# Four of sixteen mask preloads on ScalarE, filler matmuls in the first five turns, and a new order of the turn

## The reference

```python
x = x + _L0_attn_ref(_layernorm(x), Wq, Wk, Wv, ...)          # delta rule, gates, output gate
x = x + _L0_xattn_ref(_layernorm(x), ctx_1024, ctx_1024, mask, Wq, Wk, Wv, Wo)
x = x + _L0_ffn_ref(_layernorm(x), clip_x, clip_down, w_gate, w_up, w_down)
# inside _L0_xattn_ref:
scores = jnp.einsum('bhqd,bhkd->bhqk', Q, K) / np.sqrt(16)
scores = jnp.where(mask == 0, -jnp.inf, scores)
out = jnp.einsum('bhqk,bhkd->bhqd', softmax(scores), V)
```

## Time and profile before

| | us |
|---|---|
| median of 3 runs | 1278.31 (1277.05 to 1282.93) |
| the profiled execution, own time | 1273.96 |
| its span, first to last instruction | 1272.2 |
| PE busy | 1071.3 (84%) |
| DVE busy | 986.7 (78%) |
| ACT busy | 749.2 (59%) |
| POOL busy | 641.7 (50%) |

### The profile page before, as it was taken

One profiled execution on the slowest core, in us unless ns is written; L12 is line 12 of the kernel. 1 busy time (PEld: TensorE's weight loads), 2 busy tenths in 40 slices (PEclk: granted clock), 3 DMA queues, 4 the chain that ended last, 5 costly groups with the idle time before them and its releaser, 6 DMA issues. The chain is left out here.

```text
span 1272.2 us, 27987 instructions
## 1 busy us (share of the span) xinstructions
PE 1071.3 (84%) x8552; PEld 806.0 (63%) x8626; DVE 986.7 (78%) x2955; ACT 749.2 (59%) x1456; POOL 641.7 (50%) x2360
## 2 busy tenths in 40 slices
PE   5888988684677789999999999999999987875755
PEld 4767766683556567777777777777777645443224
DVE  4989988685766869788888888888888776834985
ACT  5877877432343435675666567566656544444766
POOL 4777775405334744565566556556655654101007
PEclk9988889895557869999999999999999998997989
DMA  6667666546021434353353445335343442205007
GB/s 183 214 199 231 197 208 204 180 90 173 34 84 50 121 88 127 105 150 114 93 151 110 132 123 157 115 94 150 109 138 85 145 103 59 76 26 190 1 1 232
DMA packets 159829, 160.31 MB, mean 126 GB/s; under 512 B 65320, under 2 KB 126656, under 8 KB 159680
## 3 DMA queue, kind: packets, MB, share of 16 engines
q1 hardware_dynamic: 155552, 157.47, 41.7%
q10 hardware_dynamic: 4128, 1.05, 0.4%
HBM read 96.34 MB, written 61.87 MB: 124 GB/s over the span
## 5 line engine op out<-in xcount | busy, mean ns | idle before, releaser
L2142 DVE CUSTOM_DVE_ANT_0 x_psA<-x_psA,x_mask_q 128x256 f32<-128x256 f32 x496 | 201.1, 447 | 82.5 <-PE x_psA L1431 59.2
L1694 ACT ACTIVATE x_PT<-x_psB 128x512 f32<-128x512 f32 x240 | 143.2, 596 | 140.8 <-PE x_psB L1458 133.8
L314 DVE SCALAR_TENSOR_TENSOR a_conv<-a_ps_proj,taps,a_conv 128x253 f32<-128x253 f32 (+2 forms) x288 | 114.9, 470 | 12.5 <-ACT a_conv L381 12.5
L537 PE MATMUL a_ps_proj<-a_hT,wqkv 128*128 128x256 f32 x384 | 104.8, 421 | 11.0 <-DVE a_conv L314 7.8
L1431 PE MATMUL x_psA<-x_Ks,x_Qs 96*128 96x256 bf16 x496 | 97.8, 279 | 13.0 <-DVE x_maxima L2142 12.8
L1458 PE MATMUL x_psB<-x_Qs,x_Ks 98*128 98x256 bf16 x480 | 92.7, 274 | 7.3 <-ACT x_PT L1694 2.5
L537 PEld LDWEIGHTS a_ps_proj<-a_hT,wqkv 128*128 128x128 f32 x384 | 77.1, 212 | 30.2 <-issue 15.9
L2142 DVE DVE_READ_ACCUMULATOR2_ANT x_maxima<- 128x1 f32 x512 | 72.2, 141 | 0.0
L1455 PE MATMUL x_psB<-x_mask_k,x_ident_bf 128*128 128x512 bf16 x167 | 64.8, 388 | 8.5 <-ACT x_PT L1694 7.5
L1472 PE MATMUL x_psO<-x_PT,x_V 128*32 128x256 f32 x1024 | 70.3, 393 | 1.6 <-ACT x_PT L1694 1.6
L1431 PEld LDWEIGHTS x_psA<-x_Ks,x_Qs 96*128 96x128 bf16 x496 | 41.4, 101 | 47.0 <-DVE x_maxima L2142 26.8
(11 more groups left out here) (383 smaller groups left out, 3262.5 us busy)
## 6 DMA issues: line engine op xcount, KB each, us to landing
scratch_keypack<-a_keypack SPq DMA_DIRECT2D x16, 768.0 KB, 4.2
c_keypack<-scratch_keypack SPq DMA_DIRECT2D x16, 768.0 KB, 4.9
x_Ks<-scratch_k_parts SPq DMA_DIRECT2D x192, 64.0 KB, 2.7
matrix<-scratch_taps_copies SPq DMA_DIRECT2D x32, 256.0 KB, 4.0
scratch_k_parts<-x_parts_k SPq DMA_DIRECT2D x32, 192.0 KB, 2.3
scratch_q_parts<-x_parts_q SPq DMA_DIRECT2D x32, 192.0 KB, 2.3
x_Qs<-scratch_q_parts SPq DMA_DIRECT2D x32, 192.0 KB, 3.0
a_x_in<-in_x SPq DMA_DIRECT2D x16, 256.0 KB, 3.9
```

Of the source, the lines that this page charges most:

```text
L314: nc.vector.scalar_tensor_tensor(acc, ps_proj[PROJ_BANK[p]][:, c, 0:L - j], taps[:, p, c, TAPS - 1 - j:TAPS - j], acc, ALU.mult, ALU.add). ...
L537: last = nc.tensor.matmul(ps_proj[PROJ_BANK[p]][:, o], wqkv[:, p, c, o * P:(o + 1) * P], hT[par][:, c], start=c == 0, stop=c == FC - 1)
L1694: nc.scalar.activation(PT[:, k % (2 * GROUP)], bank_B(b, k)[0], ACT.Exp, scale=XD ** -0.5).then_inc(pexp_ready, 1)
L2142: last = nc.vector.tensor_tensor_reduce(bank_A(b, k)[0][:, s], bank_A(b, k)[0][:, s], mask_q[:, t], 1.0, LOWEST, ALU.add, ALU.max, maxima[ ...
```

## The change

Three edits, all in `phase_cx`:

1. `MASKED_BY_ACT` becomes (3, 7, 11, 15). For batches 0 to 13 the L1455 matmul of these four heads is left out, and ACT copies the mask into psB (`kB3`, `kB7`, `kB11`, `kB15`).
2. PE gets filler: the operations `hot0` to `hot13` multiply the identity (read as bf16) by itself, 512 columns, into the bank psO, whose content nobody reads in those turns. `HOT[b][i]` says how many matmuls `hoti` issues for batch b; there are 134 in all, for b below 5. By turn they are 3 in turn 0, then 28, 30, 24 and 40, and 9 in turn 5, ahead of the first `pv0`. They wait for nothing, and nothing waits for them.
3. `C_ORDER` is a new list. All engines' orders change. Some operations get another stage number because the list is cut at another place (`gram0` is now the first of turn n+1 where it stood late in turn n).

```diff
-C_ORDER = [(2, "rv"), (3, "osum3"), (4, "scale"), (5, "mA10"), (2, "delta"), (1, "invx"), (5, "mA11"), (1, "invq"),
...
+C_ORDER = [(2, "r1"), (0, "invb"), (4, "scale"), (3, "mixa"), (5, "mA8"), (4, "oF"), (4, "klow"), (3, "mixb"), (4, "rstdx"),
...
+           (1, "gram0"), (6, "sB10"), (5, "sA10"), (1, "hot11"), (2, "out"), (1, "hot12"), (6, "sB11"), (5, "sA11"),
+           (6, "pv1"), (5, "sA12"), (1, "hot13"), (0, "hot0"), (6, "sB12"), (1, "gram1"), (0, "hot1"), (5, "sA13"),
+           (6, "sB13"), (6, "pv2"), (6, "sB14"), (3, "oT8"), (1, "p1"), (5, "sA14"), (0, "hot2"), (3, "og1"), (5, "sA15"),
+           (6, "sB15"), (4, "vproj"), (5, "maxT"), (6, "pv3"), (4, "sA0"), (0, "hot3"), (3, "og2"), (3, "ctxT"), (4, "Q1st"),
...
+           (4, "sA4"), (6, "wop"), (0, "hot4"), (1, "sqv"), (2, "gelu1"), (5, "eB0"), (5, "eB1"), (6, "ofc"), (3, "khigh"),
+           (5, "eB2"), (3, "oTc"), (5, "kB3"), (5, "eB3"), (1, "ua0"), (5, "eB4"), (1, "w0"), (2, "exp"), (5, "eB5"),
...
+           (2, "logits"), (4, "sA5"), (5, "sB4"), (1, "b0"), (0, "hot5"), (0, "hot6"), (7, "tuh"), (5, "sB5"), (1, "c0"),
+           (0, "hot7"), (5, "sB6"), (1, "state"), (0, "hot8"), (4, "sA6"), (0, "hot9"), (5, "pv0"), (4, "sA7"), (1, "rhs1"),
+           (3, "xT"), (5, "sB7"), (4, "sA8"), (1, "a1"), (3, "qproj"), (5, "sB8"), (1, "b1"), (4, "sA9"), (5, "sB9"),
+           (0, "hot10"), (1, "c1"), (4, "K1st"), (3, "K0st"), (1, "uc0"), (1, "S"), (5, "eB6"), (5, "kB7"), (3, "xTc"),
...
+HOT = ((2, 0, 0, 0, 0, 0, 0, 0, 0, 1, 0, 0, 1, 0),
+       (3, 0, 4, 1, 6, 0, 0, 8, 1, 0, 4, 0, 0, 4),
+       (7, 0, 0, 0, 2, 3, 4, 0, 6, 0, 4, 0, 0, 0),
+       (0, 3, 0, 3, 4, 0, 2, 3, 0, 6, 3, 0, 0, 8),
+       (0, 6, 0, 8, 0, 2, 7, 3, 0, 1, 5, 0, 1, 8))
 
-MASKED_BY_ACT = ()
+MASKED_BY_ACT = (3, 7, 11, 15)
...
+                elif op[:3] == "hot" and b < len(HOT):
+                    pair = ident[:].bitcast(BF16)
+                    for _ in range(HOT[b][int(op[3:])]):
+                        nc.tensor.matmul(psO[:], pair[:, 0:P], pair.unsqueeze(1).broadcast_to([P, 2, L]),
+                                         start=True, stop=True, skip_group_check=True)
```

More of the change, by code:

```diff
@@ L784 @@
 NVB = 2
-C_ORDER = [(2, "rv"), (3, "osum3"), (4, "scale"), (5, "mA10"), (2, "delta"), (1, "invx"), (5, "mA11"), (1, "invq"),
-           (1, "att0"), (4, "oF"), (4, "klow"), (4, "rstdx"), (7, "rstdb"), (4, "qlow"), (3, "ostat"), (5, "mA12"),
[10 rows of a table removed]
-           (3, "st_qp"), (2, "ld_x"), (3, "ld_Q0"), (2, "ld_c"), (1, "ld_hT"), (3, "statx"), (4, "mA5"), (2, "pr1"),
-           (2, "pr2"), (4, "mA6"), (2, "pr3"), (1, "r1"), (0, "invr"), (4, "mA7"), (3, "xnx"), (2, "mixa"), (4, "mA8"),
-           (2, "mixb"), (2, "mixc"), (2, "mix"), (3, "qrest"), (4, "mA9"), (2, "osum"), (5, "sB4"), (1, "c0"), (4, "sA6"),
[9 rows of a table removed]
+C_ORDER = [(2, "r1"), (0, "invb"), (4, "scale"), (3, "mixa"), (5, "mA8"), (4, "oF"), (4, "klow"), (3, "mixb"), (4, "rstdx"),
+           (3, "mixc"), (4, "qrest"), (3, "mix"), (7, "rstdb"), (5, "mA9"), (3, "osum"), (3, "osum3"), (2, "sums0"),
[15 rows of a table added]
+           (2, "ld_x"), (1, "ld_hT"), (3, "st_kp"), (3, "ld_K0"), (3, "st_qp"), (0, "ld_vs"), (3, "proj"), (5, "sB3"),
[8 rows of a table added]
+HOT = ((2, 0, 0, 0, 0, 0, 0, 0, 0, 1, 0, 0, 1, 0),
[4 rows of a table added]
 LOWEST = -3.0e38
-MASKED_BY_ACT = ()
+MASKED_BY_ACT = (3, 7, 11, 15)
 def phase_cx(nc, sems, dram, keep, ident, used, early):
```

## The result

The changed kernel takes 1265.89 us (median of 12 runs, 1257.55 to 1271.04); the kernel before, in 12 runs beside it, 1277.66 us. The ratio is 0.9905, with a 95% interval from 0.9877 to 0.9933. So 12 us were gained where 26.6 were forecast. The profiled execution took 1270.57 us, with a span of 1268.8.

A forecast was written before the change was run, and what follows sets the result against it. The prediction took PE's work to bound the steady turn, and hand-offs between engines, with PE at a low clock, the ramp. Masks 10.6, filler 12 and order 4 us saved gave 1278.31 - 26.6 = 1251.7, rounded to 1252 us; range 1236 to 1276.

The forecast's parts named there:

- Edit 1, the price: Mask matmuls on PE: each one left out saves 0.22 us from start to start, 0.88 us a turn.
- Edit 1, the sum: Masks from ScalarE: 9.7 us over 11 full turns plus a third of 2.6 us, 10.6 us saved in all.
- My count of chains: Ahead of sB3, sB7, sB11, sB15: PE's work between scores covers exponential and copy, 4.1 to 2.6 us against 1.9 to 2.6.
- `proj` to `xT`: Tightest link found in the new order: at least 7.1 us against 7.0 us of PE work, perhaps 0.1 to 0.5 us a turn.
- Edit 2: Filler in the ramp: a higher clock saves 18 us, 6 us of filler is not covered, net 12 us saved.
- Rival B: Only the steady part gains, the ramp keeps its length over DVE, POOL and ACT: 1267, up to 1272 us; chance 0.18.
- E: Filler doesn't lift the clock, its matmuls run at 0.43 us each on PE's queue: 1296 us, slower; chance 0.08.
- C: Most of the ramp's PE time was on the path, pipeline shallower by all 11 us: 1230 us; chance 0.07.
- Edit 3: New order: a shallower pipeline saves 4 of 11 us in ramp and tail; bounds 11 us saved, 4 us lost.
- The sum: Whole kernel: 10.6 + 12 + 4 = 26.6 us saved, from 1278.31 to 1251.7 us, rounded to 1252.
- rival D: Steady turn stays at 44.5 us, a late link or copy stalling PE 0.9 us a turn: 1272 to 1284 us; chance 0.09.
- What the profile was to show: Steady turn 43.6 to 43.9 us with PE busy over 98%; ramp clock near 1.0, about 170 instead of 184.7 us.

The follow-up runs named there:

- e16: The kernel before in its old order, with ScalarE writing the masks of heads 1, 3, 9, 11 and 190 filler matmuls: 1250.27 us, ratio 0.9787.
- e7: The kernel before in its old order with 190 filler matmuls alone, all masks from PE: 1260.8 us, ratio 0.9894.
- e1: The changed kernel with MASKED_BY_ACT empty, new order and filler kept: 1267.46 us, ratio 0.9944.
- e2: The changed kernel without any filler matmul, new order and ScalarE's masks kept: 1275.32 us, ratio 1.0009.
- e3: The kernel before with the new order alone, neither ScalarE's mask copies nor filler: 1281.39 us, ratio 1.0071.
- e9: The changed kernel with no mask at all, neither matmul nor copy, for heads 3, 7, 11, 15 of batches 0 to 13: 1270.51 us.
- e4: The kernel before in its old order, with ScalarE writing the masks of heads 3, 6, 9, 11, no filler: 1268.01 us, ratio 0.9963.
- e5: The kernel before in its old order, with ScalarE writing the masks of heads 3, 6, 9, 11 and 190 filler matmuls: 1250.57 us, ratio 0.9828.
- e17: The kernel before in its old order, with ScalarE writing the masks of heads 1, 3, 6, 9, 11 and filler: 1251.0 us, ratio 0.9795.

## Why the prediction was right or wrong

**What bounds the kernel: right, but one sentence claimed more than it could.** "In the steady part the sum of PE's work is the turn" holds for the kernel before to within the 1.9 us counted above. It doesn't follow that the sum less 0.88 is the next turn. PE busy for 43.96 of 44.5 us says that nobody is late by much, not by how little the others are in time. Here several hand-offs turned out to have less room than the work that was taken away ahead of them.

The reading of the ramp had a slip too: the 41.0 us of its first window begin 4 us ahead of the first evacuation, and the turn took 37.0 us.

**Edit 1, the price: right.** 0.22 us from start to start is confirmed: e16 gives 0.84/4 = 0.21 us a matmul where no wait follows. The figure of the Trainium skill (TensorE: Matmul & The Clock Gate, section Back-to-back issue gap), 131 ns for a matmul with 512 columns in a sustained stream, would give 0.52 us a turn; the measurement decides against it. The same section of the Trainium skill has about 216 ns for such a matmul taken alone at the upper clock, and that is what the runs show even in a stream: twelve filler matmuls of e7, each with its weight load, take 2.76 us, so (2.76 - 0.38)/11 = 0.216 us from start to start.

```profile
398.25 2.76 PE L1516 MATMUL x_psO<-ident 128*128 128x512 bf16 x12
```


**Edit 1, the sum: wrong.** This is the first of two steps that failed: it counted the whole start-to-start time of the four matmuls and put the waiting that would take its place at nothing. 0.88 us a turn and 10.6 us in all became 0.34 us a turn and 5 us (changed kernel against e1), or 8 us by e2 against e3, each give or take 4.5; the turn is the firmer measure. Of the missing 0.54 us, 0.30 are waits at `sA12` and `sA8`, for VectorE's maxima and not for ScalarE's copy; the rest is spread over smaller ones. My count of chains was made for the copies alone, and those did fit, as e9 shows. `proj` to `xT`, the tightest link in my list, is indeed one of the two: the last step of POOL's square root starts at 757.57 and takes 0.20 us, `xn` starts at 757.81, and what stands behind `xn` on VectorE makes PE wait 0.15 us, at `sA8` and not at `xT`. The link through `out` and `delta` to `mA11` I didn't count. "0.1 to 0.5 us a turn" for stalls stood in the text, but it was not taken off the sum.

**Edit 2: right, on the low side.** 12 us forecast, 15.3 in the ramp (e2 against changed), 11.7 with e3 against e1, and by the ratios 13 and 16 us. Of PE's time at the lower level I expected 31 to 42 us to go. Real work in the ramp took 138.41 us in e2 (no filler) and, with the filler's 34.6 us of busy time in this stretch taken off, 99.5 in the changed kernel: 39 us less. So about 39% of it (15.3 us) came off the ramp after the filler's own cost; I had said a half less 6 us. The wait of POOL for DVE's sums, 20.7 us in the earlier trace rows, is 12.4 us now, in the window 333 to 370 us:

```profile
POOL c_stat_v L1783 <- DVE c_sums L1980: 12.4, 1, 12.4
```

Not all of that is the filler's doing: e2, which has none, shows 15.2 us there. Rival B, that the ramp keeps its length because POOL and DVE hold it, falls by the 15 us between e2 and the changed kernel, and E with the clock. C fell on the masks and the order. Its sum was also off: its text takes all 11 us of the shallower pipeline, its sum adds 8; with 11 it gives 1227.

**Edit 3: wrong, by more than edit 1.** This is the second step that failed. Forecast 4 us saved, at worst 4 lost; measured 9 us lost, with an interval from 6 to 12 (e3). The other pairs of the two orders agree in kind, though their heads or their filler differ as well: by the ratios the new order is behind by 6 us with the masks (e2, e4), by 6 with the filler (e1, e7) and by 10 with both (changed, e5). Two parts of the step failed. The saving of a shallower pipeline isn't there: the ramp is 194.0 us against 193.1 to 195.9, the tail 185.4 against 182.7 and 183.8. And "a new order can only stall PE or not" was costed at nothing, though it stalls: 0.16 us a turn, 3.0 us in the steady part, at `ctxT` (0.27) and `sB6` (0.15). The depth was also read from a row that the window had cut: 748.78 is the fourth of `kproj`'s eight matmuls, and the first starts at 748.14, so the stretch before was 21.2 us and not 20.5. These 3 us and perhaps 2 of the tail are found; the rest of the 9 isn't. In the profile of e3 5 us more lie ahead of the first cut (294.4 against 289.5), in code that no kernel here changes. Over all profiles that cut lies at 285.9 to 301.2 us, with a mean of 294 in ten kernels of the new order and 292 in ten of the old, which is no difference beyond their scatter. I leave it open.

**The sum.** The estimate by the Trainium skill's price, "5 us higher", set 7.3 us against 12.3, while the sum had entered 10.6; it should have said 4. By the ratios, -5 to -8 us for the masks, -13 to -16 for the filler and +9 for the order give about -12: the result. Of the 15 us missing, 13 are the order's and the others the masks', less what the filler gave beyond its forecast. The time, 1265.89, lies within the range given, nearest to rival B's 1267, but for another reason: B lets the ramp stay and the turn shrink, and the chip did the opposite. What happened in the steady part is the mechanism of rival D (a late link eats the matmul's time), at 0.5 us a turn instead of 0.9.

**What the profile was to show.** Clock near 1.0 in the ramp: 0.82 to 0.88, then 1.00, right in kind. A ramp of about 170 instead of 184.7 us, 15 less: it is 17.7 us shorter by the cut used here, near enough. A turn of 43.6 to 43.9 us: 44.3, wrong. PE busy for over 98%: 43.58/44.30 = 98.4%, right, and it shows how little that says.

The mechanisms forecast do give the forecast time in the old order: e16 has the masks at heads with room, the filler and no new order, and gains 0.0213 of 1276.19, 27 us. It is also the fastest kernel of this study, with e17 and e5 too close to be told from it. But its 27 us are made of other terms than the forecast's 10.6 + 12 + 4: its profile is shorter by 17.2 us in the ramp, 7.2 in the steady part and 1.0 in the tail. That the total agrees is in part luck.

## What to carry to other kernels

An instruction taken off the busiest engine is worth its start-to-start time only where that engine doesn't wait for another soon after; before counting it, read from the timeline when the next operand is ready, for each place. If an order is changed together with the work, measure the order alone, and choose the places of an edit in the order that exists before making a new one for it. Where TensorE idles in pieces at the lower clock, matmuls into an idle bank ahead of the waiting steps were worth 13 to 17 us here in either order.

## What the runs showed of the hardware that was not expected

Some filler was enough for the clock: in the first turn of the ramp, cut at the same steps, the granted clock is 0.50 before (289.5 to 326.5 us, PE busy for 20.88) and 0.83 after (301.2 to 332.9 us, PE busy for 18.60, of which 8.38 are 28 filler matmuls). The same filler gave 0.90 in the ramp of e16 (178.7 us) and 0.95 in that of e17 (172.8 us), whose turns differ by one mask matmul of PE. The kernel before has 195.9 and 193.1 us in two profiles. So one profile tells a ramp to several us at best.

After some bf16 scores the next f32 step starts 0.32 us later and not 0.22, for example in e9, whose rows stand above: `sA11` starts at 723.53 and `pv1` at 723.85, while `sB11`, at 723.31, is 0.22 us ahead of `sA11`. Not every such pair shows it: in the earlier trace rows the f32 step at 751.36 follows its scores after 0.22 us. The cause is not shown. By the count above, some ten such places make up half of the 1.9 us by which a turn of the kernel before exceeds the sum of its steps' shortest times. No run took one away.
